# Moving VectorE's router places and row normalisation around the first mixer halves, and preparing the first scan chunk piece by piece, in a two-layer recurrent kernel

## The reference, cut to what matters

```python
xn = _layernorm(x)
s = _L0_attn_ref(xn, ...)          # gated linear recurrence over T
g = _silu(_L0_ffn_ref(xn, ...))    # top-1 of 4 experts
x = x + s * g
xn = _layernorm(x)
s = _L1_attn_ref(xn, ...)          # selective scan, 16 states x 512 channels
g = _silu(_L1_ffn_ref(xn, ...))    # binarised linear
x = x + s * g

# L0 mixer: f = sigmoid(xn Wf + b); z = (xn Wz) * sigmoid(xn Wzg)
#   h = f * h + z ; gated = silu(xn Wga) * (xn Wgb) * h ; y = gated Wout + b
# L1 mixer, per step:
delta = softplus(dt @ W_dt + b_dt)
dA = exp(delta[..., None] * A)
state = dA * state + (delta * u)[..., None] * B[:, None, :]
y = einsum('bdn,bn->bd', state, C)
```

## Time and profile before

| | |
|---|---|
| median of 3 runs | 1496.92 us (1496.7 to 1498.08) |
| profiled execution, its own time | 1499.23 us |
| its span | 1497.4 us |
| TensorE / VectorE / ScalarE / GpSimd busy | 94% / 68% / 60% / 62% |
| mean granted TensorE clock | 0.984 of full |
| stages | router to 54 us, mixer to 216, experts to 600, ramp to 651, scan to the end |

### The profile page before, as it was taken

The page is one execution under the profiler, slowest core; times in us unless marked ns, Lnnn a source line. Parts: engine busy times, 40 slices in busy tenths (PEclk is TensorE's granted clock), DMA queues, the critical chain, the costliest instruction groups (busy, mean ns, idle before and its releaser), DMA issues.

```text
span 1497.4 us, 24190 instructions
## 1 busy us (share of the span) xinstructions
PE 1407.2 (94%) x9074; PEld 1127.6 (75%) x9104; DVE 1017.8 (68%) x1341; ACT 891.6 (60%) x1463; POOL 928.9 (62%) x473
## 2 busy tenths in 40 slices
PE   5899999999999999779899999999999999999986
PEld 2445559999999998347678877778788788777885
DVE  6555543332323323469898898998998998989885
ACT  3211121111111111389899989989899999899880
POOL 4422211222222222058989999999989989899994
PEclk9999999999999999779999999999999999999999
DMA  9911126666767663111121120211211201212111
GB/s 304 392 57 56 56 85 254 242 266 230 263 248 260 253 251 126 33 46 41 43 71 44 43 85 30 71 57 44 85 43 33 97 30 43 71 44 66 48 56 43
DMA packets 53283, 172.70 MB, mean 115 GB/s; under 512 B 6063, under 2 KB 32303, under 8 KB 48310
## 3 DMA queue, kind: packets, MB, share of 16 engines
q1 hardware_dynamic: 46038, 150.22, 28.4%
q0 software_dynamic: 7136, 21.01, 4.2%
HBM read 141.78 MB, written 31.00 MB: 115 GB/s over the span
## 4 chain that ended last, share of the span: by engine, by line
PE 54%; ACT 14%; POOL 14%; DVE 9%; issue 7%; DMA 1%; SPq 0%; POOLq 0%; DVEq 0%; ACTq 0%
PE bank L1366 17%; PE bank L1312 9%; POOL hst L647 8%; PE bank L1379 8%; ACT dA L838 6%; ACT dbuT L829 5%; PE bank L1539 5%; DVE hst L1218 4%; PE bank L1556 4%; POOL dbuT L622 4%; PE bank L1499 1%; PE bank L1341 1%; PE bank L1449 1%; PE bank L1438 1%; PE bank L1431 1%
## 5 line engine op out<-in xcount | busy, mean ns | idle before, releaser
L1218 DVE TENSOR_TENSOR_SCAN hst<-dA,carry,bank 128x512 f32<-128x512 f32 x512 | 631.2, 1268 | 49.3 <-PE bank L1539 46.5
L647 POOL TENSOR_TENSOR hst<-hst,c_bc 128x2048 f32<-128x2048 f32 x127 | 578.2, 4559 | 19.5 <-DVE hst L1218 5.6
L838 ACT ACTIVATE dA<-delta,negA 128x512 f32<-128x512 f32 x512 | 356.9, 711 | 7.9 <-DVE hst L1218 7.7
L1539 PEld LDWEIGHTS bank<-ident,dbuT 128*128 128x128 f32 x2048 | 242.8, 142 | 150.7 <-issue 74.6
L1539 PE MATMUL bank<-ident,dbuT 128*128 128x128 f32 x2048 | 315.5, 277 | 26.2 <-DVE hst L1218 20.8
L1556 PE MATMUL bank<-ident,hst 128*128 128x128 f32 x2032 | 295.2, 274 | 9.7 <-POOL hst L647 9.7
L829 ACT ACTIVATE dbuT<-duT,bT 128x512 f32<-128x512 f32 x384 | 272.2, 709 | 2.1 <-PE bank L1539 2.1
L1366 PEld LDWEIGHTS bank<-f_sb,w_gu 128*128 128x128 f32 x2240 | 255.6, 192 | 2.7 <-ACT f_sb L714 1.0
L1366 PE MATMUL bank<-f_sb,w_gu 128*128 128x128 f32 x2240 | 256.0, 275 | 0.7 <-ACT f_sb L714 0.7
L1556 PEld LDWEIGHTS bank<-ident,hst 128*128 128x128 f32 x2032 | 236.2, 141 | 12.8 <-POOL hst L647 12.1
L585 POOL TENSOR_TENSOR x_sb<-x_sb,neg_half 128x1 f32<-128x1 f32 x35 | 23.1, 659 | 261.6 <-DVE x_sb L1068 261.6
(11 more groups left out here) (196 smaller groups left out, 1724.7 us busy)
## 6 DMA issues: line engine op xcount, KB each, us to landing
w_gu<-in_w_gu SPq DMA_DIRECT2D x35, 2048.0 KB, 7.3
c_bc<-c_rows SPq DMA_DIRECT2D x64, 512.0 KB, 3.7
sorted_x<-sg_a SPq DMA_DIRECT2D x12, 387.0 KB, 11.6
x_sb<-sorted_x SPq DMA_DIRECT2D x35, 129.0 KB, 7.2
x_sb<-in_x SPq DMA_DIRECT2D x8, 512.0 KB, 7.7
w_d<-in_w_d SPq DMA_DIRECT2D x1, 4096.0 KB, 20.1
x_mix<-x_sb SPq DMA_DIRECT2D x1, 4096.0 KB, 31.0
x_mix<-rt SPq DMA_DIRECT2D x8, 512.0 KB, 2.9
```

Source lines behind the costliest of these rows:

```text
L647: pool.tensor_tensor(h[:], h[:], c, ALU.mult).then_inc(hc_ready, 1)
L838: act.activation(dA[:, at % DA_BUFS, :], delta[q % B][:, d, :], ACT.Exp, scale=negA[:, d, n:n + 1]).then_inc(dA_ready, 1)
L1218: v.tensor_tensor_scan(h[:, d, :], dA[:, at % DA_BUFS, :], bank[4 + u % 2][:], carry1[q % B][:, n, d:d + 1], ALU.mult, ALU.add).then_inc(s ...
L1539: ins = pe.transpose(bank[4 + u % 2][:, i * P:(i + 1) * P], dbuT[(DS * q + n) % DBU_BUFS][:, i, d * P:(d + 1) * P], ident[:])
```

## The change

VectorE's row places become a function and are run in the mixer's chunk 0 between its halves. The rows of chunk 0 are made behind both its halves, those of chunk 1 between its halves; later chunks keep them in front. For this the mixer's chunk 1 is unrolled on VectorE. In the ramp, TensorE does two z parts, half of DT, then the turn of the next chunk's input, and the rest of DT; the other z parts lie between the later steps, and turn 0 of du ahead of B's. Softplus is issued interleaved over the blocks with the Relu (as add and max) on VectorE; the last du block is made by VectorE; the decays of units 0 and 1 are made between the copies of duT; of state 0's four pieces ScalarE makes two and VectorE two.

```diff
@@ -105,7 +105,9 @@
         "OUT1", "BT", "DUT0", "DUT1", "DUT2", "DUT3", "Z0", "Z1", "Z2", "Z3", "XN0", "XN1")
 CLAIMS = sorted(JOBS, key=lambda name: CLAIMED[name])
 FIRST_CLAIMS = {"X0": 0, "X1": 1, "X2": 2, "X3": 3, "Z0": 6, "Z1": 7, "Z2": 4, "Z3": 5, "DT": 0, "DL0": 1, "DL1": 2,
-                "DL2": 3, "DL3": 0, "BC": 6, "BT": 7, "DUT0": 1, "DUT1": 2, "DUT2": 3, "DUT3": 0, "XN0": 6, "XN1": 7}
+                "DL2": 3, "DL3": 0, "XN0": 6, "XN1": 7, "BC": 6, "BT": 7, "DUT0": 1, "DUT1": 2, "DUT2": 3, "DUT3": 0}
+FIRST_PIECES = 2
+
 
 FIRST_TURN, BANK_A, BANK_B = -2, 6, 7
 
@@ -337,6 +339,9 @@
         c_loaded = [sem(f"c_loaded{i}") for i in range(2)]
         dA_ready = sem("dA_ready")
         dbuT_act = sem("dbuT_act")
+        dbuT_first = sem("dbuT_first")
+        relu_ready = sem("relu_ready")
+        du_last = sem("du_last")
         dbuT_pool = sem("dbuT_pool")
         dbu_full = sem("dbu_full")
         scan_done = sem("scan_done")
@@ -603,7 +608,7 @@
 
 
             def make_du(t, d):
-                pool.wait_ge(xc_ready, DB * (t + 1) + DB)
+                pool.wait_ge(xc_ready, DB * (t + 1) + (DB if t >= 0 else d + 1))
                 wait_freed(pool, t, f"DL{d}")
                 pool.tensor_tensor(du[:, d, :], delta[(t + 1) % B][:, d, :], xc[:, d, :], ALU.mult).then_inc(du_ready, 1)
 
@@ -618,11 +623,13 @@
 
                 wait_past(pool, dbu_full, unit(q, DB * (n - DBU_BUFS) + DB))
                 wait_freed(pool, q - 1, "DUT3")
+                if q == 0:
+                    wait_freed(pool, -1, "BT")
                 at = DS * q + n
                 pool.tensor_tensor(dbuT[at % DBU_BUFS][:], duT[q % B][:],
                                    bT[q % B][:, :, n:n + 1].broadcast_to([P, TPC, DI]), ALU.mult).then_inc(dbuT_pool, 1)
 
-            for d in range(DB):
+            for d in range(DB - 1):
                 make_du(-1, d)
             def last_state(h):
                 for d in range(DB // 2):
@@ -824,6 +831,8 @@
                     return
                 if p == 0:
                     wait_freed(act, q - 1, "DUT3")
+                    if q == 0:
+                        wait_freed(act, -1, "BT")
                 if i == 0:
                     wait_past(act, dbu_full, unit(q, DB * (n - DBU_BUFS) + DB))
                 act.activation(dbuT[(DS * q + n) % DBU_BUFS][:, i, :], duT[q % B][:, i, :], ACT.Copy,
@@ -831,7 +840,9 @@
 
             def decay(q, u):
                 n, d = divmod(u, DB)
-                if u == 0:
+                if q == 0 and n == 0:
+                    wait_freed(act, -1, f"DL{d}")
+                elif u == 0:
                     wait_freed(act, q - 1, "DL3")
                 at = unit(q, u)
                 wait_past(act, scan_done, at - DA_BUFS + 1)
@@ -844,17 +855,47 @@
             for d in range(DB):
                 silu_conv(-1, d)
             act.preload_act_table_set("natural_log_exp_and_others")
-            for d in range(DB):
-                softplus(-1, d)
-            for d in range(DB):
-                turn_du(-1, d)
-            for p in range(AHEAD):
+
+            def first_abs(d):
+                wait_full(act, -1, f"DL{d}")
+                act.activation(soft[:, d, :], place(-1, f"DL{d}")[:], ACT.Abs,
+                               bias=cols1[:, d, KC + 1:KC + 2]).then_inc(soft_step, 1)
+
+            def first_exp(d, step):
+                act.wait_ge(soft_step, step)
+                act.activation(soft[:, d, :], soft[:, d, :], ACT.Exp, scale=-1.0).then_inc(soft_step, 1)
+
+            def first_ln(d, step):
+                act.wait_ge(soft_step, step)
+                act.activation(soft[:, d, :], soft[:, d, :], ACT.Ln, bias=one[:]).then_inc(soft_ready, 1)
+
+            first_abs(0)
+            first_abs(1)
+            first_exp(0, 1)
+            first_abs(2)
+            first_exp(1, 2)
+            first_ln(0, 3)
+            first_abs(3)
+            first_exp(2, 4)
+            first_ln(1, 5)
+            first_exp(3, 6)
+            first_ln(2, 7)
+            first_ln(3, 8)
+            turn_du(-1, 0)
+            decay(0, 0)
+            turn_du(-1, 1)
+            turn_du(-1, 2)
+            decay(0, 1)
+            turn_du(-1, 3)
+            for p in range(TPC - FIRST_PIECES):
                 spread_du(0, p)
             for q in range(CHUNKS):
                 for u in range(UNITS):
-                    decay(q, u)
+                    if q > 0 or u > 1:
+                        decay(q, u)
                     if u + AHEAD < UNITS:
-                        spread_du(q, u + AHEAD)
+                        if q > 0 or u + AHEAD >= TPC:
+                            spread_du(q, u + AHEAD)
                     elif q + 1 < CHUNKS:
                         spread_du(q + 1, u + AHEAD - UNITS)
                     slot(q, u)
@@ -960,28 +1001,30 @@
             for e in range(NE):
                 then(v.tensor_tensor_scan(cum[:, :, e], rs[:, 3, :], tot[:, :, e], 0.0, ALU.mult, ALU.add))
 
-            cnt = cum[:, TILES - 1, :]
...
+            def place_rows():
+
+                cnt = cum[:, TILES - 1, :]
...
+                v.tensor_copy(eid[:], eidf[:, :, NE - 1]).then_inc(eid_ready, 1)
 
 
             def mixer(c, b):
@@ -993,17 +1036,26 @@
                     ins.then_inc(v_l0, 1)
                     return c * L0_STEPS + k[0]
 
-                wait_past(v, scattered, 64 * c)
-                wait_past(v, mix_added, 2 * c)
-                for i in range(TPC):
-                    t = c * TPC + i
-                    v.tensor_scalar(xn_st[:, i, 0:D], x_sb[:, bass.ds(t, 1), :], mean0[:, bass.ds(t, 1)],
-                                    rstd0[:, bass.ds(t, 1)], ALU.subtract, ALU.mult)
-                v.tensor_copy(xn_st[:, :, D], top_w[:, bass.ds(c * TPC, TPC)])
-                v.tensor_copy(xn_st[:, :, D + 1].bitcast(U32), id_u[:, bass.ds(c * TPC, TPC)])
-                v.tensor_copy(idx4[:], dest_u[:, bass.ds(c * TPC, TPC)]).then_inc(st_ready, 1)
+                def rows():
+                    wait_past(v, scattered, 64 * c)
+                    wait_past(v, mix_added, 2 * c)
+                    for i in range(TPC):
+                        t = c * TPC + i
+                        v.tensor_scalar(xn_st[:, i, 0:D], x_sb[:, bass.ds(t, 1), :], mean0[:, bass.ds(t, 1)],
+                                        rstd0[:, bass.ds(t, 1)], ALU.subtract, ALU.mult)
+                    v.tensor_copy(xn_st[:, :, D], top_w[:, bass.ds(c * TPC, TPC)])
+                    v.tensor_copy(xn_st[:, :, D + 1].bitcast(U32), id_u[:, bass.ds(c * TPC, TPC)])
+                    v.tensor_copy(idx4[:], dest_u[:, bass.ds(c * TPC, TPC)]).then_inc(st_ready, 1)
+
+                early = c if isinstance(c, int) and c < 2 else None
+                if early is None:
+                    rows()
                 for s in range(SB):
                     r = 10 * c + 5 * s
+                    if early == 0 and s == 1:
+                        place_rows()
+                    if early == 1 and s == 1:
+                        rows()
                     v.wait_ge(proj_ready, r + PROJ_Z + 1)
                     v.wait_ge(sig_ready, 6 * c + 3 * s + 2)
                     w1 = chain(v.tensor_tensor(z_sb[:, s, :], bank[2 + PROJ_Z][:], sg_z[:, s, :], ALU.mult))
@@ -1022,6 +1074,9 @@
                     v.tensor_tensor(gated[:, s, :], og_sb[:, s, :], h_sb[:, s, :],
                                     ALU.mult).then_inc(gated_ready, 1)
                 assert k[0] == SB * L0_SB == L0_STEPS
+                if early == 0:
+                    rows()
+                    v.wait_ge(st_ready, 1)
                 for h in range(2):
                     v.wait_ge(mix_ready, 2 * c + h + 1)
                     if h == 0:
@@ -1033,8 +1088,10 @@
             for b in range(B):
                 wait_past(v, gated_ready, SB * CPB * b)
                 v.memset(carry0[:], 0.0).then_inc(carry_set, 1)
-                mixer(CPB * b, b)
-                with v.Fori(CPB * b + 1, CPB * (b + 1)) as c:
+                unrolled = 2 if b == 0 else 1
+                for c in range(CPB * b, CPB * b + unrolled):
+                    mixer(c, b)
+                with v.Fori(CPB * b + unrolled, CPB * (b + 1)) as c:
                     mixer(c, b)
 
 
@@ -1195,17 +1252,42 @@
             for d in range(DB):
                 for part in range(KC - 1):
                     conv(-1, d, part)
-            for i in range(TPC):
-                z_part(-1, i)
+            def first_relu(d, step):
+                M = place(-1, f"DL{d}")
+                v.wait_ge(soft_step, step)
+                v.tensor_scalar(M[:], M[:], cols1[:, d, KC + 1:KC + 2], 0.0, ALU.add, ALU.max).then_inc(relu_ready, 1)
+
+            def first_delta(d):
+                v.wait_ge(relu_ready, d + 1)
+                make_delta(-1, d)
+
+            def first_piece(i):
+                v.tensor_scalar(dbuT[0][:, i, :], duT[0][:, i, :], bT[0][:, i, 0:1], None,
```

(72 more changed lines are left out.)

27 lines of the change are left out of this document (19 added, 8 removed).

## The result

The changed kernel takes 1486.31 us (median of 4 runs, 1486.15 to 1486.68) against 1496.81 (1496.65 to 1498.08): ratio 0.992, 95% interval 0.9908 to 0.9932, so 10.5 us less. Forecast was 11.6 less, 1485.3, with a range of 1482.8 to 1490.2. Both parts work; the part in the ramp is worth a little less than forecast, and how much one sees of it depends on where TensorE's clock falls in an execution.

The account below looks back on a forecast made before the run. It took the kernel as TensorE-bound in mixer and experts, then a serial ramp and a scan stage with nearly all engines full. 5.7 + 5.9 = 11.6 us off 1496.92 gives 1485.3 us, range 1482.8 to 1490.2.

Parts of the forecast that it names:

- Part one: Mixer's first chunk: TensorE no longer waits for VectorE's row places and rows, nor runs at half clock after; 5.7 us won.
- The moved steps: Mixer: rows, expert numbers, weight loads and scatters come later but stay hidden; zero cost taken, 1.4 us as bound.
- The scatter: Mixer chunk 0: GpSimd's last issue at 73.8, landing at 76.6 by the median or 82.6 at worst; zero cost taken.
- if VectorE waits between the halves of chunk 1: Mixer chunk 1: a stated sign of being wrong; no idle time of VectorE for the scatter was forecast there.
- The limit I worked out: Mixer chunk 1: chunk 0's scatter may land until 80.0 us without cost.
- Part two: Ramp into the scan layer: reordered work on TensorE, ScalarE and VectorE brings the next chunk's first convolution step 5.9 us sooner.
- the scan's first turn: Ramp's end: TensorE's four matmuls ahead of the first scan, taken at 1.1 us, the lower clock level, against 0.66.
- The rule that I weighed against it: Ramp: activity releases TensorE's throttle; with full clock the scan starts 5.9 us sooner, not 5.4; faster rival 1483.3, chance 0.08.
- The seven later chunks repeat the same order and keep the shift: Scan stage: the head start of 5.9 us from the ramp lasts through the seven later chunks.
- VectorE is full from there on: Scan stage behind 660 us: VectorE has no idle time, busy 4.00 of 4 us, so the ramp's shift passes on.
- a sign of being wrong: Scan stage: the 11.6 us distance between old and new traces shrinks inside the first scan chunk or drifts later.
- the term that I put at 5.9: Ramp's gain: ScalarE's queue before the next chunk's first x block ends at 651.4 instead of 657.35, 5.9 us won.

Follow-up runs that it names:

- e4: Kernel before the change, with four idle matmuls put into TensorE's wait for the first half's product in mixer chunk 0: 1495.03 us, ratio 0.9988.
- e3: Kernel before the change with only the ramp's part of the change, old mixer kept: 1492.75 us, ratio 0.997.
- e5: Changed kernel, but mixer chunk 1 makes its rows in front of both halves, like later chunks: 1494.53 us against 1496.95 for the kernel before.
- e2: Kernel before the change with only the mixer's part of the change, old ramp kept: 1490.43 us against 1497.41, ratio 0.9958.
- e1: Kernel before the change, profiled once more without any edit: 1498.28 us over 11 runs.
- e9: Changed kernel without further edit, timed again on another chip: 1487.06 us against 1498.33 for the kernel before, ratio 0.9929.
- e6: Changed kernel, but the decays of units 0 and 1 come behind the pieces, not between the copies of duT: 8.9 us less than the kernel before.
- e7: Changed kernel, but ScalarE makes all four pieces of state 0 and VectorE none: 9.4 us less than the kernel before.
- e8: Changed kernel, but softplus's Relu stays on ScalarE, directly behind each block's Abs: 8.3 us less than the kernel before.
- e12: Changed kernel, but TensorE makes all four z parts at the ramp's start and none in later gaps: 1488.83 us.
- e10: Changed kernel, du turns 2 and 3 ahead of the last z part; a decay, VectorE's pieces and a z-copy wait also moved: 1485.40 us, ratio 0.9916.
- e11: Changed kernel, but GpSimd makes the last du block as before, instead of VectorE: 1486.44 us.

## Why the prediction was right

**Part one.** Forecast 5.7 us as 3.79 of wait and 1.96 of half clock. O to P is shorter by 5.6. e4 shows the two terms apart: 1.7 of clock with the wait left in, so 3.9 for the wait. The clock's term is not a constant of the kernel: the same wait in e3 had 1.4 us more of it behind it. The margin of the second half's gating, put at 0.2 us, is 0.23.

**The moved steps.** The expert numbers and weight loads are hidden, P to H is 535.7 in both. The scatter was a wrong detail, and by my own signs ("if VectorE waits between the halves of chunk 1") it counts against the prediction: I had no idle time of VectorE in chunk 1, with a landing at 76.6 by the median row; it landed at 78.9, 6.4 us behind its last issue at 72.5, with the DMA engines nearly full until 78 us. The limit I worked out, 80.0, held, so the cost is zero as taken. e5 shows what that limit protects: 8 us.

**Part two, up to its end.** Between the profiles of before and after, DT comes 2.25 sooner (forecast 2.1), the first scan 5.9 (5.4), the convolution step 6.1 (5.9). So close an agreement is in part luck, because before had drawn a slow ramp. VectorE's copy of DT stands 23.1 us behind H in before, but 22.3 and 21.9 in e2 and e4 with the same old order, and 20.9 in after. Averaged over the four profiles with the old ramp (before, e1, e2, e4) and the four with the new one (after, e9, e3, e5), the first scan comes 4.9 sooner and the convolution step 5.3. That ScalarE's queue and not the first scan ends the ramp, as I took it, is shown by e6, where the two moved in opposite directions.

One row was misjudged: I took 1.1 us for the scan's first turn by the old ramp, and it took 0.66 (638.89 to 639.55). The rule that I weighed against it is of the Trainium skill, TensorE: Matmul & The Clock Gate, section on the HAM clock gate: activity releases the throttle. The trace of after fits it: TensorE had waited four times, 3.6 us in all, ahead of the turns of B and du, waits there for none of them now, and its turns ran at 2.4 GHz. But it does not decide the case. The same new ramp in e3 has 0.84 for the first turn, e7 has 1.29 at the low clock, and the old ramp in e2 0.87; which of them an execution gets does not follow from the order of the work alone.

**Part two, behind its end.** "The seven later chunks repeat the same order and keep the shift" held to 0.1 us from T0 to T6. "VectorE is full from there on" did not hold inside chunk 0: the 6.1 us at C are 5.5 at T0, and the distance between the two traces shrinks there from 12.1 to 11.5, which I had named as a sign of being wrong. From C to T0 the executions take between 26.7 and 28.1 us (26.9 in before, 27.4 in after, 26.7 in e2, 28.1 in e4). VectorE is busy for 26.6 to 26.8 of them in every profile, so what differs is its waiting. At least a part of a stretch of half clock lies in there each time, at another place, and the chain of waits in after runs over TensorE's turns and x matmuls from 652 to 661 us. So a shift at C isn't passed on whole, as e6 and e8 show too. Over the same four and four profiles H to T0 is 77.1 and 72.2, which is 4.9 for the term that I put at 5.9: 0.6 of the missing 1.0 is missing at C already, the rest behind it. This is the term that was too large. I had worked it out from the rows of one execution that was 2.3 us above the median.

5.6 + 4.9 = 10.5 is what the first comparison shows. Over the same profiles T6 to T7 is 0.8 shorter on average too, and with it the sum is 11.3, what e9's comparison shows. It isn't known which value of T6 to T7 the unprofiled executions had, so whether a part of the medians' difference lies there stays open.

**The sum against the profile.** The spans differ by 13.0 because the profiled execution of before, 2.3 above its median, held a low clock where the last two chunks meet and the long value in the ramp. I had carried that 2.3 over to the profile after as if it belonged to the kernel: 1487.6 for the profiled execution's own time, measured 1486.15. The forecast of the median did not add it, but took its ramp from the same slow execution.

## What to carry to other kernels

A serial chain on one engine ahead of a bound engine costs the wait and then the slow clock behind it; look which of its steps the bound engine waits for and move the others behind it, but follow each resource they hold (here the rows' buffer and its scatter) to the next iteration. In a ramp, ask at each engine's idle stretch what of the later work already has its operands: putting z parts into gaps helped (e12), and an order with the last one behind the last turns, with three small moves beside it, gained 1.5 us more (e10). Steps of half a microsecond can't be priced by medians that scatter by two; distances between marks within a profile can, once the stretches of low clock are known.

## What the runs showed of the hardware that I had not expected

The clock's falls are not a fixed feature of the code. The same old ramp, to its first scan, took 43.3 us in two profiles and 41.6 to 41.7 in two others, and the meeting of chunks 6 and 7 takes 98.8 or 100.4 us and nothing else in fourteen profiles. The part of the 2 to 4 us scatter of a kernel's executions that these profiles can account for lies in these places.

VectorE's product of two SBUF tensors (L1283) took 1.38 us, and 1.37 in e10, with GpSimd's product of the same kind beside it, against 0.69 for VectorE's products with one operand in a bank, beside GpSimd or not. GpSimd's two took 2.51 us as if alone, and the three in e11 3.74. No experiment was made on this, but the traces show which of the two gives way. At the end of every kernel here VectorE makes two more such products, of the last states, in the trace of after:

```profile
L1307 DVE TENSOR_TENSOR hst<-hst,c_bc x2: 679/3382/6084, 1456.8 to 1462.8; 128x512 f32<-128x512 f32 x2
...
1458.64 1.28 POOL L620 TENSOR_TENSOR g_out<-g_out,x 128x512 f32<-128x512 f32 x1
1459.88 2.50 POOL L638 TENSOR_TENSOR hst<-hst,c_bc 128x512 f32<-128x512 f32 x2
```

The first takes 6.08 us and ends at 1462.92, 0.55 behind the last of GpSimd's products (1462.38); the second, with GpSimd idle, takes 0.68. The product of L1283 ends 0.55 behind GpSimd's second (633.88) as well. In all 23 such meetings, of 14 profiles, VectorE's product ends 0.55 us after GpSimd's row of products does, and GpSimd's keep their time. So these two engines do not share the time here: VectorE waits until GpSimd is through. In the ramp this was hidden (e11). At the kernel's end VectorE's last product is over 1.15 us behind GpSimd's (1463.53 against 1462.38); by my estimate from these rows that much stands to be won there, which was not tried.
